# GpSimd's queue in a masked-attention and graph-layer kernel: a block's power goes ahead of the casts that wait for transposes, and the first four casts go out while x is still coming

## The chip, the cores and the metric

The kernel runs on one core of one Trainium2 chip. The metric is the device time of one execution in microseconds (us). Before the change it is 515.58 us, the median of three runs (515.1 to 516.22).

## What is computed

The reference takes x (4096 x 128, float32), a 0/1 matrix adj (4096 x 4096, float32), a scalar beta and a weight (128 x 128):

```python
def L0(x, adj, beta):                     # N = 4096, D = 128
    norm2 = jnp.linalg.norm(x, axis=1, keepdims=True)
    cos = beta[0] * (x @ x.T) / (norm2 @ norm2.T + 1e-07)
    masked = cos + (1.0 - adj) * -1000000000.0
    P = jax.nn.softmax(masked, axis=1)
    return P @ x
def L1(x, edge_index, weight):
    return jnp.matmul(edge_index, jnp.matmul(x, weight))
x = layernorm(x + L0(x, adj, beta))
x = layernorm(x + L1(x, adj, weight))
```

## The kernel before

The 4096 rows are cut into 8 blocks (NB) of 512. For block b the scores against all 4096 columns are made in 16 pairs m = 0 to 15, a pair being two tiles of 128 columns. A pair passes through the engines like this:

- TensorE multiplies the unit rows in three half-precision products for each tile (`scores`, L854 to L856).
- ScalarE takes the exponential (`exp_pair`, L424).
- VectorE masks it with the bytes of adj (`mask_pair`, L639).
- ScalarE writes the upper half-precision part (`split_hi`, L433), and VectorE the rest (`split_lo`, L647).
- TensorE weighs the rows of x with both, three pairs behind the scores (`weigh`, L877 and L881; LAG = 3). A ring of four buffers holds the pairs.

VectorE works in an order written out by hand. In block b it also does the work on the rows of block b-1: it reads the sums at pair 3 (`read_out`, L685), adds the residual rows at pairs 4 and 5 (`residual`, L698, which waits for the transfer of `xres`), takes moments at 6 and 7, makes the variance at pair 8 (`norm_stats`, whose last instruction is L677), and at pair 10 the shift (`row_shift`, L709), which waits for the inverse root of the variance (`rstd_done`).

That inverse root is a `pow` on GpSimd (`power`, L376). GpSimd works in the order of its program as well, and has three kinds of work in it:

- Casts of adj. Each block of adj is four pieces of 512 rows x 1024 columns. `cast(k)` with k = 4b + c issues a DMA from float32 to one byte, DRAM to DRAM (L353). Piece 0 is cut in three (`cast_first(0)` to `cast_first(2)`, L356), which hold the columns of pair 0, pair 1, and pairs 2 and 3. SyncE then issues the DMA that transposes the piece into SBUF (L258 for the first three, L264 for the others). `cast(k)` first waits until the transpose of piece k-2 has landed, so two pieces are under way at a time.
- The powers: four at the start for the norms of x (`inverse_norms(c)`, L360; x comes in four chunks), and one for each block of rows (L376).
- For each block the lower part of the new rows (`x1_split`, L388), after ScalarE's upper part (L469).

At the start VectorE sums the squares of a chunk of x, GpSimd takes the power, VectorE makes the unit rows (`unit_rows`, L530), TensorE turns them, and the pairs of block 0 follow. A mask at the first pair of a piece waits for the piece's transpose. SyncE has its own order: in round b the transposes of block b+1, then the store of the new rows of block b-1 and the load of `xres` for block b (L287), then the store of the parts (L284).

After the last block come the second layer's products (L935, L945), some 125 us, in which no cast is left.

Of the kernel before, what the change touches and what calls it, by code (L numbers as in the profile page):

```python
# [21 lines left out]
def resnorm_graph_kernel(nc, x, adj, beta, weight, x1_dram, x1p_dram, q_dram, adj8_dram, out):  # L22
# [8 lines left out]
    NB = N // BI  # L31
# [9 lines left out]
    NC = 4  # L41
    CT = NT // NC
    MP = 4
# [7 lines left out]
    with ExitStack() as ctx:  # L51
# [3 lines left out]
        def sem(name):  # L55
            return ctx.enter_context(nc.semaphore(name))
# [62 lines left out]
        x_in = [sem(f"x_in{c}") for c in range(NC)]  # L119
# [76 lines left out]
        def piece(v, b, c):  # L196
            return v[b, :, c * PW:(c + 1) * PW]

        def first_piece(v, f):

            c, n = FIRST[f]
            return v[0, :, c * 2 * P:(c + n) * 2 * P]

        def pieces_in(b, c):
            return 16 * (b if c == 0 else b + 1)
# [21 lines left out]
        def chunk(c):  # L227
            return slice(c * CT, (c + 1) * CT)
# [107 lines left out]
        @block.gpsimd  # L336
        def _(pool):
            nc.gpsimd.memset(ident[:, :], 0.0).then_inc(consts, 1)
            nc.gpsimd.memset(xaug[:, :, D:D + 1], 1.0).then_inc(consts, 1)
            nc.gpsimd.memset(half_pow[:, :], -0.5).then_inc(consts, 1)  # L340
            nc.gpsimd.memset(ext[:, :], 0.0).then_inc(consts, 1)
            pool.wait_ge(consts, 4)
            nc.gpsimd.affine_select(out=ident[:, :], in_=ident[:, :], compare_op=ALU.not_equal, fill=1.0,
                                    base=0, pattern=[[-1, P]], channel_multiplier=1).then_inc(consts, 1)

            def cast(k):

                b, c = divmod(k, MP)
                if k < 3:
                    pool.wait_ge(first_in[k], 16)  # L350
                else:
                    pool.wait_ge(piece_in[(k - 2) % MP], pieces_in(*divmod(k - 2, MP)))
                pool.dma_start(piece(adj8_v, b, c), piece(adj_v, b, c)).then_inc(piece_cast[c], 16)  # L353

            def cast_first(f):
                pool.dma_start(first_piece(adj8_v, f), first_piece(adj_v, f)).then_inc(first_cast[f], 16)  # L356

            def inverse_norms(c):
                pool.wait_ge(n2_done, c + 1)
                nc.gpsimd.tensor_tensor(rn[:, chunk(c)], n2[:, chunk(c)], half_pow[:, chunk(c)],  # L360
                                        ALU.pow).then_inc(rn_done, 1)

            inverse_norms(0)

            pool.wait_ge(x_in[NC - 2], 16)
            cast_first(0)
            inverse_norms(1)
            cast_first(1)
            inverse_norms(2)
            cast_first(2)  # L370
            inverse_norms(3)
            for k in range(1, 2 * MP + 2):
                cast(k)
            def power(done, o, n):
                pool.wait_ge(stats_done, done)
                nc.gpsimd.tensor_tensor(rstd[:, o:o + n], rstd[:, o:o + n], half_pow[:, 0:n], ALU.pow).then_inc(rstd_done, 1)  # L376

            for b in range(NB - 1):

                for c in range(2, MP):  # L380
                    if b + 2 < NB:
                        cast((b + 2) * MP + c)
                power(b + 1, 0, IT)
                for c in range(2):
                    if b + 3 < NB:
                        cast((b + 3) * MP + c)
                pool.wait_ge(x1_hi, b + 1)
                nc.gpsimd.tensor_tensor(x1p[:, :, 1, :], x1[:, :, :], x1p[:, :, 0, :],  # L388
                                        ALU.subtract).then_inc(x1_split, 1)
            power(NB, 0, IT)  # L390
            for r in range(NB - 1):
                power(NB + r + 1, IT * (r % 2), IT)
            for half in range(2):
                power(2 * NB + half, IT + half * HT, HT)
# [598 lines left out]
```

## Time and profile before

| | |
|---|---|
| median of the runs | 515.58 us |
| the profiled execution | 515.68 us, its span 513.8 us |
| granted TensorE clock, mean | 0.984 of full speed |
| busy: TensorE, VectorE, ScalarE, GpSimd | 469.7, 380.6, 314.2, 64.8 us |
| chain that ended last | PE 66%, DMA 20%, DVE 4%, issue 4%, ACT 3%, POOL 1% |
| cast transfers | 31 of 512 KB written, median 11.1 us from issue to landing |
| time of the DMA engines | casts 39.5%, SyncE's and the rest of that queue 30.2% of 16 engines' span |

In the profile PE is TensorE, DVE is VectorE, ACT is ScalarE, POOL is GpSimd and SP is SyncE. The span runs from the first to the last instruction. The time of a run is the span and some 2 us around it.

### The profile page before, as it was taken

What the parts mean: (1) busy time and instruction counts of PE and PEld (TensorE: products, weight loads), DVE (VectorE), ACT (ScalarE), POOL (GpSimd) and SP (SyncE); (2) the same over time, 40 slices, a digit from 0 to 9 for tenths busy, and PEclk for the clock granted to TensorE, in tenths of its full rate; (3) what the DMA queues carried; (4) which work ended last, traced back from release to release, by engine and by line L of the source; (5) the groups of instructions that cost most, each with busy time, mean ns of one, the idle gap of its engine ahead of it and who ended that gap; (6) DMA issues with size and microseconds to landing.
All of it is one profiled execution on the core that took longest, in us unless ns stands there. A gap on an engine that the chain in (4) does not pass through costs nothing.

```text
span 513.8 us, 8872 instructions
## 1 busy us (share of the span) xinstructions
PE 469.7 (91%) x3491; PEld 305.1 (59%) x3491; DVE 380.6 (74%) x630; ACT 314.2 (61%) x358; POOL 64.8 (13%) x71
## 2 busy tenths in 40 slices
PE   0866999957999999999999999999999999999995
PEld 0533676635676666766666767666665455544584
DVE  4976989928999999999999999999994022212253
ACT  3665888828879978988988997898891000000000
POOL 3500000010101201201120210110101000000011
PEclk9988999997999999999999999999999999999998
DMA  5899899999999999999989979520024101111111
GB/s 189 62 101 127 86 122 115 137 127 115 172 127 135 131 136 118 131 169 115 112 171 114 105 152 104 93 74 7 1 51 156 63 5 37 41 43 41 42 37 46
DMA packets 101690, 50.20 MB, mean 98 GB/s; under 512 B 69376, under 2 KB 98208, under 8 KB 101664
## 3 DMA queue, kind: packets, MB, share of 16 engines
q0 software_dynamic: 17952, 16.78, 39.5%
q1 hardware_dynamic: 83424, 33.05, 30.2%
q8 instruction: 11, 0.18, 0.1%
q14 instruction: 15, 0.12, 0.1%
q10 hardware_dynamic: 288, 0.07, 0.1%
HBM read 77.40 MB, written 22.82 MB: 195 GB/s over the span
## 4 chain that ended last, share of the span: by engine, by line
PE 66%; DMA 20%; DVE 4%; issue 4%; ACT 3%; POOL 1%; POOLq 0%; ACTq 0%; DVEq 0%
PE psum L935 21%; PE psum L877 16%; DMA adj_bytes<-in_adj 12%; PE psum L881 8%; DMA adjT<-adj_bytes 7%; PE psum L854 7%; PE psum L856 7%; PE psum L855 7%; DVE E L639 2%; ACT E L424 1%; PE psum L945 1%; DMA adjT<-in_x 1%; ACT eh L433 1%; DVE el L647 1%; POOL rn L360 1%
## 5 line engine op out<-in xcount | busy, mean ns | idle before, releaser
L877 PE MATMUL psum<-xaug,eh 128*128 128x257 f16 x1024 | 187.9, 277 | 22.5 <-DVE el L647 15.4
L424 ACT ACTIVATE E<-psum,sc 128x1024 f32<-128x1024 f32 x128 | 154.1, 1204 | 54.8 <-PE psum L856 50.6
L881 PE MATMUL psum<-xaug,el 128*128 128x129 f16 x1024 | 178.7, 223 | 0.0
L639 DVE SCALAR_TENSOR_TENSOR E<-E,adjT 128x1024 f32<-128x1024 f32 x128 | 160.0, 1250 | 21.1 <-ACT E L424 13.0
L647 DVE SCALAR_TENSOR_TENSOR el<-E,eh 128x1024 f16<-128x1024 f32 x128 | 156.5, 1223 | 0.1
L433 ACT ACTIVATE eh<-E 128x1024 f16<-128x1024 f32 x128 | 134.0, 1047 | 3.8 <-DVE E L639 3.8
L877 PEld LDWEIGHTS psum<-xaug,eh 128*128 128x128 f16 x1024 | 100.3, 99 | 52.3 <-DVE el L647 16.9
L935 PE MATMUL psum<-adjT,uT 128*128 128x512 fp8e4 (+1 forms) x576 | 112.1, 355 | 0.0
L881 PEld LDWEIGHTS psum<-xaug,el 128*128 128x128 f16 x1024 | 101.4, 99 | 13.4
L854 PE MATMUL psum<-uT 128*128 (+1 forms) x256 | 98.4, 384 | 0.0
L855 PE MATMUL psum<-uT 128*128 (+1 forms) x256 | 97.8, 382 | 0.0
L856 PE MATMUL psum<-uT 128*128 (+1 forms) x256 | 97.5, 381 | 0.0
L935 PEld LDWEIGHTS psum<-adjT,uT 128*128 128x128 f16 x576 | 56.4, 98 | 53.0
L501 ACT ACTIVATE E<-psum 128x512 f32<-128x512 f32 x7 | 4.2, 597 | 88.0 <-PE psum L935 88.0
L792 DVE TENSOR_TENSOR E<-psum,E 128x512 f32<-128x512 f32 x7 | 4.8, 690 | 68.1 <-PE psum L945 68.1
L376 POOL TENSOR_TENSOR rstd<-rstd,half_pow 128x4 f32<-128x4 f32 (+1 forms) x17 | 22.2, 1304 | 186.1 <-DVE rstd L677 186.1
L353 POOL DMA_DIRECT2D adj_bytes<-in_adj x31 | 19.6, 631 | 192.1 <-DMA adjT<-adj_bytes 192.1
L856 PEld LDWEIGHTS psum<-uT 128*128 128x128 f16 x256 | 25.3, 99 | 31.0 <-issue 1.4
L854 PEld LDWEIGHTS psum<-uT 128*128 128x128 f16 x256 | 25.4, 99 | 17.9 <-issue 0.7
L855 PEld LDWEIGHTS psum<-uT 128*128 128x128 f16 x256 | 25.3, 99 | 16.4 <-issue 0.5
L460 ACT ACTIVATE x<-h,shift,rstd 128x128 f32<-128x128 f32 x32 | 15.2, 482 | 16.6 <-DVE shift L709 16.6
L388 POOL TENSOR_TENSOR x1p<-x,x1p 128x512 f16<-128x512 f32 x7 | 12.4, 1764 | 58.6 <-ACT x1p L469 58.6
(71 smaller groups left out, 159.9 us busy)
## 6 DMA issues: line engine op xcount, KB each, us to landing
adj_bytes<-in_adj POOLq DMA_DIRECT2D x31, 512.0 KB, 11.1
adjT<-in_x SPq DMA_DIRECT2D x4, 512.0 KB, 8.6
xres<-in_x SPq DMA_DIRECT2D x8, 256.0 KB, 5.3
q_row<-norms SPq DMA_DIRECT2D x8, 256.0 KB, 4.9
x_rows<-x SPq DMA_DIRECT2D x8, 256.0 KB, 3.6
E<-x_rows SPq DMA_DIRECT2D x8, 256.0 KB, 3.0
out<-E SPq DMA_DIRECT2D x16, 128.0 KB, 2.2
x_parts<-x1p SPq DMA_DIRECT2D x7, 256.0 KB, 5.5
```

What stands on the lines that cost most here:

```text
L353: pool.dma_start(piece(adj8_v, b, c), piece(adj_v, b, c)).then_inc(piece_cast[c], 16)
L376: nc.gpsimd.tensor_tensor(rstd[:, o:o + n], rstd[:, o:o + n], half_pow[:, 0:n], ALU.pow).then_inc(rstd_done, 1)
L424: nc.scalar.activation(E[:, m % RING, :, :], S[m % 2], ACT.Exp, bias=col(C_BB), scale=col(C_BS)).then_inc(e_done, 1)
L433: nc.scalar.activation(eh[:, m % RING, :, :], E[:, m % RING, :, :], ACT.Copy, scale=ECAST).then_inc(hi_done, 1)
L639: nc.vector.scalar_tensor_tensor(out=e, in0=e, scalar=EPRE, in1=mask_bytes(b, m), op0=ALU.mult, op1=ALU.min).then_inc(masked, 1)
L647: nc.vector.scalar_tensor_tensor(out=el[:, s, :, :], in0=E[:, s, :, :], scalar=ECAST, in1=eh[:, s, :, :], op0=ALU.mult, op1=ALU.subtract). ...
L854: nc.tensor.matmul(o, hj, hi, start=True, stop=False)
L855: nc.tensor.matmul(o, hj, li, start=False, stop=False)
L856: last = nc.tensor.matmul(o, lj, hi, start=False, stop=True)
L877: return nc.tensor.matmul(O[t][:, 0:XC], eh[:, s, a, cols], xaug[:, j, :], start=start, stop=stop)
L881: return nc.tensor.matmul(O[t][:, 0:D + 1], el[:, s, a, cols], xaug[:, j, 0:D + 1], start=False, stop=False)
L935: last = nc.tensor.matmul(out, x1p_all[:, j, part * D:(part + 1) * D], adj_cols(r, j, cols), start=j == 0 and part == 0, stop=j == NT - 1 ...
```

## The change

Two places of GpSimd's program change, and nothing else.

At the start GpSimd waits for the second chunk of x where it had waited for the third, and this wait and two of the first casts now stand ahead of the first power. The third of the first casts and `cast(1)` follow that power; `cast(1)` no longer waits for the transpose of the pair-1 columns.

In the loop over the blocks the power of block b stands ahead of `cast` for pieces 2 and 3 of block b+2, where it had stood behind them. The casts themselves, their order and their waits stay.

```diff
             def cast(k):
                 b, c = divmod(k, MP)
-                if k < 3:
+                if k == 2:
                     pool.wait_ge(first_in[k], 16)
-                else:
+                elif k > 2:
                     pool.wait_ge(piece_in[(k - 2) % MP], pieces_in(*divmod(k - 2, MP)))
                 pool.dma_start(piece(adj8_v, b, c), piece(adj_v, b, c)).then_inc(piece_cast[c], 16)
...
+            pool.wait_ge(x_in[1], 16)
+            cast_first(0)
+            cast_first(1)
             inverse_norms(0)
-
-            pool.wait_ge(x_in[NC - 2], 16)
-            cast_first(0)
+            cast_first(2)
+            cast(1)
             inverse_norms(1)
-            cast_first(1)
             inverse_norms(2)
-            cast_first(2)
             inverse_norms(3)
-            for k in range(1, 2 * MP + 2):
+            for k in range(2, 2 * MP + 2):
                 cast(k)
...
             for b in range(NB - 1):
-                for c in range(2, MP):
-                    if b + 2 < NB:
-                        cast((b + 2) * MP + c)
+
                 power(b + 1, 0, IT)
-                for c in range(2):
-                    if b + 3 < NB:
-                        cast((b + 3) * MP + c)
+                for k in range((b + 2) * MP + 2, (b + 3) * MP + 2):
+                    if k < NB * MP:
+                        cast(k)
                 pool.wait_ge(x1_hi, b + 1)
                 nc.gpsimd.tensor_tensor(x1p[:, :, 1, :], x1[:, :, :], x1p[:, :, 0, :],
                                         ALU.subtract).then_inc(x1_split, 1)
```

## Rows read from the trace of the kernel before

**Rows 1.** The waits of the whole span: engine, line, releaser, total us, times, longest.

```profile
DVE shift L709 <- POOL rstd L376: 11.4, 2, 10.3
DVE E L639 <- DMA adjT<-adj_bytes: 7.7, 1, 7.7
```

**Rows 2.** VectorE's timeline, 64 to 145 us: start, length, what, idle before.

```profile
83.87 0.75 DVE L685 TENSOR_TENSOR h<-psum,o_lo 128x256 f32<-128x256 f32 x2
...
100.98 0.16 DVE L677 TENSOR_TENSOR rstd<-tmp 128x4 f32<-128x4 f32 x1
...
115.95 0.16 DVE L709 SCALAR_TENSOR_TENSOR shift<-mean,rstd 128x4 f32<-128x4 f32 x1 [10.27 <-POOL rstd L376]
...
137.66 0.74 DVE L685 TENSOR_TENSOR h<-psum,o_lo 128x256 f32<-128x256 f32 x2
...
143.06 0.60 DVE L698 SCALAR_TENSOR_TENSOR h<-h,rden,xres 128x128 f32<-128x128 f32 x2
```

**Rows 3.** VectorE's timeline, 175 to 186 us.

```profile
180.22 0.75 DVE L685 TENSOR_TENSOR h<-psum,o_lo 128x256 f32<-128x256 f32 x2
```

**Rows 4.** GpSimd's timeline, 0 to 70 us.

```profile
9.75 1.66 POOL L360 TENSOR_TENSOR rn<-n,half_pow 128x8 f32<-128x8 f32 x1 [8.04 <-DVE n L526]
11.35 0.81 POOL L356 DMA_DIRECT2D adj_bytes<-in_adj  x1
12.19 2.32 POOL L360 TENSOR_TENSOR rn<-n,half_pow 128x8 f32<-128x8 f32 x1
...
43.50 0.62 POOL L353 DMA_DIRECT2D adj_bytes<-in_adj  x1 [15.07 <-DMA adjT<-adj_bytes]
```

**Rows 5.** The chain of work that ended last, in order of time: start, length, what.

```profile
14.48 3.90 DMA adj_bytes<-in_adj
...
24.98 10.62 DMA adj_bytes<-in_adj
35.62 7.60 DMA adjT<-adj_bytes
```

**Rows 6.** VectorE's timeline, 0 to 64 us.

```profile
14.54 1.23 DVE L530 SCALAR_TENSOR_TENSOR adjT<-adjT,rn 128x1024 f32<-128x1024 f32 x1
...
43.31 1.23 DVE L639 SCALAR_TENSOR_TENSOR E<-E,adjT 128x1024 f32<-128x1024 f32 x1 [7.67 <-DMA adjT<-adj_bytes]
```

**Rows 7.** ScalarE's timeline, 0 to 64 us.

```profile
36.97 1.20 ACT L424 ACTIVATE E<-psum,sc 128x1024 f32<-128x1024 f32 x1 [3.99 <-PE psum L856]
```

**Rows 8.** TensorE's timelines, 9 to 60 us and 100 to 125 us.

```profile
46.92 0.39 PE L877 MATMUL psum<-xaug,eh 128*128 128x257 f16 x1 [4.86 <-DVE el L647]
...
118.44 0.40 PE L877 MATMUL psum<-xaug,eh 128*128 128x257 f16 x1 [8.86 <-DVE el L647]
```

**Rows 9.** Windows: stretch, its us, busy us of each engine, granted clock, DMA share, GB/s.

```profile
10.00:28.00 18.00, 12.34 (x59) 7.70 (x59) 17.15 (x54) 13.07 (x33) 10.44 (x9) 1.00 0.78 74
28.00:60.00 32.00, 22.82 (x167) 15.33 (x168) 23.78 (x22) 20.70 (x21) 1.66 (x3) 0.89 1.07 114
47.00:50.00 3.00, 3.00 (x18) 2.21 (x19) 3.00 (x3) 1.82 (x2) 0.00 (x0) 0.50 1.09 100
```

**Rows 10.** GpSimd's timeline, 60 to 520 us.

```profile
75.74 0.61 POOL L353 DMA_DIRECT2D adj_bytes<-in_adj  x1 [12.53 <-DMA adjT<-adj_bytes]
...
95.19 0.61 POOL L353 DMA_DIRECT2D adj_bytes<-in_adj  x1 [1.16 <-DMA adjT<-adj_bytes]
...
114.87 1.04 POOL L376 TENSOR_TENSOR rstd<-rstd,half_pow 128x4 f32<-128x4 f32 x1
...
155.01 1.95 POOL L376 TENSOR_TENSOR rstd<-rstd,half_pow 128x4 f32<-128x4 f32 x1 [3.31 <-DVE rstd L677]
...
226.49 0.64 POOL L353 DMA_DIRECT2D adj_bytes<-in_adj  x1 [10.50 <-DMA adjT<-adj_bytes]
...
240.15 1.95 POOL L376 TENSOR_TENSOR rstd<-rstd,half_pow 128x4 f32<-128x4 f32 x1 [10.34 <-DVE rstd L677]
```

**Rows 11.** SyncE's timeline, 64 to 145 us.

```profile
129.49 0.43 SPq L287 DMA_DIRECT2D xres<-in_x  x1
```

**Rows 12.** The page's DMA issues: count, KB each, median us to landing.

```profile
xres<-in_x SPq DMA_DIRECT2D x8, 256.0 KB, 5.3
```

## The prediction, made before the changed kernel ran

> **What bounds the kernel now.** I read the page's chain first (TensorE 66%, DMA 20%), then the waits, then the timelines of the engines around each long one. In steady state TensorE sets the pace: the read-out of a block's sums comes at 137.66 and the next at 180.22 [rows 2, 3], so a block takes 42.56 us, 2.66 a pair. The DMA share of the chain lies all before 115 us, and two waits of VectorE stand there [rows 1]:
>
> - Stall A, in block 0: the mask of pair 4 waits 7.67 us, until 43.31, for the transpose of piece 1 [rows 6]. Its cast was issued at 24.98, took 10.62, and the transpose 7.60 [rows 5].
> - Stall B, in block 1: the shift of pair 10 waits 10.27 us, until 115.95, for the power [rows 2]. Its input had been made at 100.98. GpSimd came to it only at 114.87 [rows 10], because two casts stood ahead of it that waited for transposes. Nothing else was missing.
>
> Later blocks have neither: there GpSimd reaches the power before VectorE has the variance, and idles for it (3.31 and 10.34 us [rows 10]).
>
> **Stall B: the power first.** The price of stall B is read from the blocks, not from the wait. Between the read-outs of blocks 0 and 1 lie 137.66 - 83.87 = 53.79 us [rows 2] against 42.56 without a stall: 11.2 us. That is 8.9 us in which TensorE stood [rows 8], and a rest for the half clock behind it and a slow mask. All of it goes if the power comes in time. After the change GpSimd's casts 2 to 9 still precede this power; the last of them went out at 95.19, done by 95.8 [rows 10], and not later with a stream that starts sooner. With stall A's gain below (4.1) the variance is made at 96.9, the power is done 1.95 us later [rows 10] at 98.9, and VectorE asks for it at 105.68 - 4.1 = 101.6. Cover: 2.7 us. Gain 11.2; bounds 10.3 (the wait alone) and 11.8.
>
> The row of the power itself says something too: 1.04 us while VectorE stood waiting, 1.95 while it worked [rows 10]; I charge the longer one. The Trainium skill ("SBUF — State Buffer", section "Who interferes with whom") says that a GpSimd instruction that reads SBUF and a VectorE one with two SBUF inputs shut each other out. By it the power may wait out one mask; the cover still holds, and the sum is the same. The same page's warning, that casts issued by GpSimd can starve for descriptors while VectorE holds the pair, speaks against the first four casts; it is priced as a rival.
>
> **What the moved casts lose.** The casts now stand behind the power, so behind its wait for the variance; behind them wait the transposes and the lower part of the new rows. In blocks 1 and 2 the variance comes 15 us sooner (155.01 gives 139.7), before the next cast is free to go, so nothing is held. From block 3 it holds: cast 22 went out at 226.49, and its power runs at 240.15 - 15.3 = 224.9, done at 226.8 [rows 10]. With the stream 5 us sooner the cast could go at 221.5, so it loses some 5 us. The piece is then ready at 226.8 + 18.2 (10.62 + 7.60 [rows 5]) = 245.0. Its mask is pair 8 of block 5, two blocks and five pairs after 180.22, less 15.3: 263.3. Cost 0. If that cover were gone it would cost 5 us.
>
> **Stall A: the start.** Three terms.
>
> 1. The powers for the norms come later. The second chunk of x is there at about 9.4 (an estimate: VectorE's and ScalarE's work on it begins between 9.4 and 9.6; the first power's 9.75 bounds it from above). Then two issues of 0.81 and 0.61 to 0.7 [rows 4, 10], the first power of 1.66 [rows 4], two more issues, and the second power of 2.32 [rows 4]: 9.4 + 1.5 + 1.7 + 1.4 + 2.3 = 16.3. The second unit rows began at 14.54 [rows 6], right when that power ended. VectorE has no gap worth the name from there to pair 4, so all of block 0 starts 1.8 us later. Bounds 1.0 and 2.6 (all powers at their short, or long, length).
> 2. Piece 1 comes sooner. Its cast goes out at 13.9 instead of 24.98. The DMA engines were at share 0.78 from 10 to 28 us and at 1.07 when full [rows 9], so the idle time that can be filled is 18 x 0.29 / 1.07 = 4.9 us, and I take the whole stream 5 us sooner: piece 1 at 43.2 - 5 = 38.2. It can be more (7), since piece 1 no longer shares with piece 2 from its start. From below, 2 us, the lead of the first cast (11.35 [rows 4] to 9.4).
> 3. What is late next is not the mask's place in VectorE's order but the exponential of pair 4. It ran from 36.97 to 38.17 [rows 7], because TensorE had just come out of a wait. Shifted by 1.8 it ends at 40.0, later than piece 1. So the mask gains 43.31 - 40.0 = 3.3 and not 7.7. For TensorE: the weighing that restarted at 46.92 [rows 8] waits for three VectorE instructions of 1.2 to 1.3 us from the mask on, so without the DMA it was free at 38.2 + 3.8 = 42.0, 4.9 sooner; the 3 us at half clock (1.2 GHz) behind that pause [rows 9] cost 1.5 more; some 0.5 is given back, as VectorE, with two extra instructions for x in these pairs, is just slower than TensorE there. 4.9 + 1.5 - 0.5 - 1.8 = 4.1.
>
> Are the next pieces there? Piece 4 (block 1, pair 0) let cast 6 go at 75.74 [rows 10], so was ready at 75.45. Its mask is three pairs before 83.87, at 75.9; it had 0.4 us to spare. After: needed at 71.8, ready at 70.4. Piece 8 (block 2) was cast before 95.19, so ready by 113.4, less 5; needed at 137.66 - 15.3 - 8.0 = 114.4. From there on 42.6 us a block leave the stream ahead.
>
> `xres` of block 1's rows is the other close one. SyncE issues it behind four transposes, at 129.49 [rows 11]; after, 124.5. With the median of 5.3 [rows 12] it lands at 129.8, and the residual wants it at 143.06 - 15.3 = 127.8 [rows 2]. That is 2 us late, of which TensorE feels what exceeds the 1.4 us between VectorE's wait in stall B and its own (10.27 against 8.86 [rows 2, 8]): 0.6, and nothing if the stream gains 7. I put 0.
>
> **Sum.** 4.1 + 11.2 = 15.3 us. The profiled execution took 515.68, so 500.4; the median of the runs is 0.1 lower, which I ignore: 500.4.
>
> **Rivals.**
>
> - The stream is late again (or `xres` is). If it comes only 2 us sooner, piece 1 is ready at 41.2 (1.2 late) and piece 4 at 73.4 against 71.8; `xres` at 132.8 against 127.8, 5 late, 3.6 of them felt. Together up to 5: 501.5 to 505. For it: piece 4 had 0.4 to spare, and the three wants lie within 2 us of supply. Against: the idle DMA time at the start is there to be filled.
> - The start gains more: shift 1.0, B at its upper bound: 498.3 to 499.3. For it: pieces early; against: VectorE is full there.
> - Only one stall goes, because a new wait fills the other: gain 4.1 to 10.5, 505 to 511.5. For it only the closeness above.
> - Nothing moves: the power still stands behind something. Then 515.6. The order of the program speaks against it.
> - Slower: the fourth cast in a row doesn't leave GpSimd until room is made, the other powers stand behind it, and the start slides. Casts ahead of it were never more than two under way, so no row shows four. Held for h us, the time is 500.4 + h. It decides from h = 15.3, about when piece 1's own cast would land (13.9 + 10.62, and up to 5 for the two ahead): then 516 to 518. Against it: each issue of the trace took 0.6 to 0.8.
>
> **How the numbers follow.** Forecast with its own range 499.3 to 501.5: 0.60. Stream or `xres` late: 0.22. More at the start: 0.07. One stall only: 0.06. Nothing: 0.02. Slower: 0.03. Faster by over 0.2% (1 us, about what a measurement of this kernel can tell) 0.95, within it 0.02, slower 0.03. The range 498.3 to 505 leaves out the last three and little else.
>
> **What would show it.** Right: VectorE's wait for the power in block 1 is gone; 42.6 between all read-outs; read-out of block 0 at 79.8, of block 1 at 122.4; the second unit rows near 16.3; the mask of pair 4 waits for ScalarE and not for a DMA; the first four issues within 5 us. Wrong: a wait of a mask for a transpose at pairs 4, 12 or the first of block 1, a wait of the residual for `xres`, an issue on GpSimd over 1 us, or a power before 17 us that is longer than 2.4.

## The result, and the profile after

The changed kernel takes 507.2 us (median of 4 runs, 505.87 to 509.05) against 515.34 for the kernel before: ratio 0.9848, interval 0.9801 to 0.9894. It is faster, but by half of what was forecast (500.4), and outside the range. Run again later (experiment 8) the same program took 503.82 (502.4 to 505.02), ratio 0.9792 (0.976 to 0.9824). In both together its runs spread from 502.4 to 509.05. Two slow executions among the experiments, one of 1007.18 us in the second and one of 508.53 in the fifth, are left out of the medians and ratios given there.

The profiled execution took 508.47 us, its span was 506.7. First the waits of the whole span: engine, line, releaser, total us, times, longest. VectorE's lines after the change stand one lower than before; the power of GpSimd, L376 before, is L377.

```profile
DVE h L697 <- DMA xres<-in_x: 3.4, 1, 3.4
DVE E L638 <- DMA adjT<-adj_bytes: 2.2, 1, 2.2
```

VectorE's wait for the power in block 1 is gone [rows 1]; so is pair 4's for piece 1. Two others are new. VectorE's timeline shows where (start, length, what, idle before):

```profile
14.42 1.23 DVE L529 SCALAR_TENSOR_TENSOR adjT<-adjT,rn 128x1024 f32<-128x1024 f32 x1 [0.25 <-POOL rn L360]
...
24.98 1.23 DVE L638 SCALAR_TENSOR_TENSOR E<-E,adjT 128x1024 f32<-128x1024 f32 x1 [2.25 <-DMA adjT<-adj_bytes]
...
41.11 1.22 DVE L638 SCALAR_TENSOR_TENSOR E<-E,adjT 128x1024 f32<-128x1024 f32 x1 [3.27 <-ACT E L423]
...
80.68 0.75 DVE L684 TENSOR_TENSOR h<-psum,o_lo 128x256 f32<-128x256 f32 x2
...
123.25 0.75 DVE L684 TENSOR_TENSOR h<-psum,o_lo 128x256 f32<-128x256 f32 x2
...
133.11 0.61 DVE L697 SCALAR_TENSOR_TENSOR h<-h,rden,xres 128x128 f32<-128x128 f32 x2 [3.41 <-DMA xres<-in_x]
...
167.24 2.17 DVE L638 SCALAR_TENSOR_TENSOR E<-E,adjT 128x1024 f32<-128x1024 f32 x1 [0.27 <-ACT E L423]
...
170.47 0.74 DVE L684 TENSOR_TENSOR h<-psum,o_lo 128x256 f32<-128x256 f32 x2
...
252.43 2.65 DVE L646 SCALAR_TENSOR_TENSOR el<-E,eh 128x1024 f16<-128x1024 f32 x1
```

The read-outs of the eight blocks, before and after, are the account of the whole change:

| interval between read-outs | before | after | after, again |
|---|---|---|---|
| (read-out of block 0) | 83.87 | 80.68 | 79.55 |
| 0 to 1 | 53.79 | 42.57 | 42.57 |
| 1 to 2 | 42.56 | 47.22 | 43.17 |
| 2 to 3 | 42.57 | 43.17 | 43.33 |
| 3 to 4 | 42.57 | 43.64 | 43.17 |
| 4 to 5 | 42.57 | 43.40 | 43.58 |
| 5 to 6 | 42.57 | 42.56 | 42.57 |
| 6 to 7 | 40.49 | 40.64 | 40.45 |

Stall B gives 11.2 us, as forecast. The read-out of block 0 comes 3.2 sooner (how much of that is the start's doing, experiment 1 shows). Then 4.65 us are lost in one interval and 0.6, 1.1 and 0.8 in the next three: 7.2 us lost, against 14.4 won.

GpSimd's timeline and a line of SyncE's show what lies at these places:

```profile
98.04 1.94 POOL L377 TENSOR_TENSOR rstd<-rstd,half_pow 128x4 f32<-128x4 f32 x1 [8.97 <-DVE rstd L676]
...
144.95 1.95 POOL L377 TENSOR_TENSOR rstd<-rstd,half_pow 128x4 f32<-128x4 f32 x1 [18.74 <-DVE rstd L676]
146.88 1.31 POOL L353 DMA_DIRECT2D adj_bytes<-in_adj  x2
164.50 0.61 POOL L353 DMA_DIRECT2D adj_bytes<-in_adj  x1 [16.30 <-DMA adjT<-adj_bytes]
166.52 0.62 POOL L353 DMA_DIRECT2D adj_bytes<-in_adj  x1 [1.41 <-DMA adjT<-adj_bytes]
167.16 1.17 POOL L387 TENSOR_TENSOR x1p<-x,x1p 128x512 f16<-128x512 f32 x1
```

```profile
122.57 0.43 SPq L287 DMA_DIRECT2D xres<-in_x  x1
```

Casts 14 and 15 go out back to back at 146.88, right behind the power: neither waited for its transpose any more, they had been held. Casts 16 and 17 wait for their transposes, and the subtraction for the lower part of the new rows (L387), last in the queue, starts at 167.16. ScalarE had made the upper part, all that it needs, at 160.8. The subtraction starts 0.08 us ahead of a mask, and that mask takes 2.17 us instead of 1.22. The read-out follows at 170.47, one `split_lo` later.

In the kernel before, ScalarE itself released the subtraction in these blocks. There, too, it made a mask longer, but that mask stood 7.5 us ahead of the read-out at 180.22, and the interval was 42.57 all the same. VectorE's timeline of the kernel before:

```profile
172.68 1.83 DVE L639 SCALAR_TENSOR_TENSOR E<-E,adjT 128x1024 f32<-128x1024 f32 x1 [0.27 <-ACT E L424]
```

In the changed kernel the instructions beside the subtraction in the next three intervals took 1.82, 2.65 and 2.06 us, 0.6, 1.4 and 0.8 over the usual 1.22, and the intervals are 0.6, 1.1 and 0.8 too long.

### The profile page after: what moved, and what is told of

It is laid out like the page before. It is cut to its first block, busy times and chain, and to the rows that moved or that the text cites. A ratio compares the mean times of both kernels' runs of the same rounds, so it can differ in the third digit from the quotient of the medians.

```text
span 506.7 us, 8872 instructions
## 1 busy us (share of the span) xinstructions
PE 467.8 (92%) x3491; PEld 303.3 (60%) x3491; DVE 382.3 (75%) x630; ACT 315.2 (62%) x358; POOL 62.2 (12%) x71
## 4 chain that ended last, share of the span: by engine, by line
PE 60%; DMA 24%; DVE 7%; issue 3%; ACT 3%; SPq 1%; POOL 1%; POOLq 0%; ACTq 0%; DVEq 0%
PE psum L934 21%; DMA adj_bytes<-in_adj 15%; PE psum L876 13%; PE psum L880 7%; DMA adjT<-adj_bytes 6%; PE psum L855 6%; PE psum L854 6%; PE psum L853 6%; DVE el L646 3%; DVE E L638 2%; DMA xres<-in_x 2%; PE psum L944 1%; DMA adjT<-in_x 1%; ACT E L423 1%; ACT eh L432 1%
## 5 line engine op out<-in xcount | busy, mean ns | idle before, releaser
L880 PE MATMUL psum<-xaug,el 128*128 128x129 f16 x1024 | 176.9, 222 | 0.0
L646 DVE SCALAR_TENSOR_TENSOR el<-E,eh 128x1024 f16<-128x1024 f32 x128 | 159.1, 1243 | 0.0
L377 POOL TENSOR_TENSOR rstd<-rstd,half_pow 128x4 f32<-128x4 f32 (+1 forms) x17 | 23.1, 1359 | 246.1 <-DVE rstd L676 246.1
L831 PE MATMUL psum<-ident,adjT 128*128 128x128 f32 x32 | 6.2, 351 | 13.6 <-DVE adjT L529 13.6
```

Of the source, the lines that this page charges most:

```text
L646: nc.vector.scalar_tensor_tensor(out=el[:, s, :, :], in0=E[:, s, :, :], scalar=ECAST, in1=eh[:, s, :, :], op0=ALU.mult, op1=ALU.subtract). ...
L880: return nc.tensor.matmul(O[t][:, 0:D + 1], el[:, s, a, cols], xaug[:, j, 0:D + 1], start=False, stop=False)
```

## The experiments

All ratios are to the kernel before, run beside it on the same chip. Experiments 1, 2, 3 and 5 were run together, then 4, 6, 7 and 8, then 9 to 12. The expectations of experiments 1 and 2 speak of GpSimd's "multiply" for the lower part; it is the subtraction. The intervals given are those up to the read-out of block 6; the last one is 40.4 to 40.8 us in every trace.

**1. The loop alone.** The start is put back word for word:

```diff
-            pool.wait_ge(x_in[1], 16)
-            cast_first(0)
-            cast_first(1)
             inverse_norms(0)
-            cast_first(2)
-            cast(1)
+            pool.wait_ge(x_in[NC - 2], 16)
+            cast_first(0)
             inverse_norms(1)
...
```

> The start is that of the kernel before; only the loop over the blocks has the power ahead of four casts. Theory (the gain of stall B is given back by the residual rows' transfer and by GpSimd's multiply for the lower part falling on a full stretch of VectorE): the wait for the power in block 1 is gone, the wait of pair 4 in block 0 for its piece stays at 7.7 us, read-out of block 0 at 83.9; the residual of block 1's rows waits 2 to 6 us for its transfer (issued near 129.5, wanted near 131.9); the read-outs of blocks 3 to 5 follow each other at 43.0 to 43.7 us instead of 42.6. Time 505 to 509 us, a gain of 7 to 10. Rival (nothing is given back, the loss of the changed kernel is all in the start): no wait for the transfer, all read-outs at 42.6, time 504.2, a gain of 11.2.

506.99 us, ratio 0.9848 (0.9823 to 0.9873). Intervals 42.57, 44.05, 44.4, 43.5, 42.57, 43.57: all that stall B cost is won, and much is given back. The residual waited in three blocks, 2.16, 1.00 and 1.35 us; the load of the first was issued at 126.87, behind a stream that was late as before. The read-out of block 0 came at 80.35, not 83.9: x arrived 1.6 us sooner than in the profile of before, and pair 4 waited 5.86 us. So when x comes in scatters by 1.6 us (the first clamp of the norms ran at 9.50 before, at 7.9 in the traces of the changed kernel and of this one), and with x equally soon the old start has its read-out at 80.35, no later than the changed kernel's 80.68. None of the 3.2 us is shown to be the start's.

**2. The start alone.**

```diff
             for b in range(NB - 1):
-                power(b + 1, 0, IT)
-                for k in range((b + 2) * MP + 2, (b + 3) * MP + 2):
+                for c in range(2, MP):
+                    if b + 2 < NB:
+                        cast((b + 2) * MP + c)
+                power(b + 1, 0, IT)
+                for c in range(2):
...
```

> The start is the changed one; the loop is that of the kernel before, with two casts ahead of each power. Theory: the first mask waits some 2 us for the transpose of the first columns, read-out of block 0 comes 2 to 3 us sooner than before; casts 10 and 11 go out at 104 to 106, so the power is done near 108 and VectorE waits some 5 us for it instead of 10.3; from block 2 on all read-outs at 42.6, since GpSimd's multiply comes where it came before; time 506 to 509.5. Rival (the start gives back what it brings, and the gain of the changed kernel is the loop's alone): within 2 us of before, 513 to 515.5.

503.99 us (501.89 to 505.02), ratio 0.9802 (0.977 to 0.9833): the start alone gains about what both parts gained together (0.9848 and 0.9792). Its waits, 20 to 200 us, and GpSimd's timeline, 95 to 105 us:

```profile
DVE shift L710 <- POOL rstd L377: 2.2, 1, 2.2
DVE E L640 <- DMA adjT<-adj_bytes: 1.2, 1, 1.2
```

```profile
98.14 0.62 POOL L353 DMA_DIRECT2D adj_bytes<-in_adj  x1 [14.71 <-DMA adjT<-adj_bytes]
102.01 0.62 POOL L353 DMA_DIRECT2D adj_bytes<-in_adj  x1 [3.25 <-DMA adjT<-adj_bytes]
102.64 1.05 POOL L377 TENSOR_TENSOR rstd<-rstd,half_pow 128x4 f32<-128x4 f32 x1
```

The casts that stood ahead of the power (111.59 and 114.24 in the kernel before) go out 12 to 13 us sooner (1.6 of it is x's earlier arrival), and of stall B's 10.3 us only 2.2 are left, with the power still in its old place. The intervals are 44.3 and then 42.56 to 42.58. My expectation had 5 us left. The two parts of the change heal the same stall, and only the loop's part lengthens the blocks behind it.

**3. The residual rows' load ahead of the last transpose of a round.**

```diff
                 for c in range(MP):
...
+                    if c == MP - 1 and ahead_of_last is not None:
+                        store_x1(ahead_of_last - 1)
+                        load_xres(ahead_of_last)
                     sp.wait_ge(piece_cast[c], pieces_in(b, c))
...
```

> The changed kernel, with SyncE issuing the store of the new rows and the load of the residual rows ahead of the last of the four transposes of a round, not behind it. Theory (the residual's wait of 3.4 us and most of the 4.7 us that block 2 is too long are this transfer): no wait of the residual, read-outs of blocks 1 and 2 at 42.6 to 43.6 instead of 47.2, a gain of 3 to 4.5 us on the changed kernel, 503 to 504.5. Rival (with the wait gone the ring's slack or a late piece takes its place, or the transfer lands as late because the engines are full): a gain under 1 us, and either a wait of the residual that stays, or a mask that waits for a transpose in block 2.

502.08 us, ratio 0.9759 (0.9735 to 0.9784). No wait of the residual; the second interval is 42.7. The later ones stay long (43.28, 42.88, 43.32): the second loss is another.

**4. The subtraction ahead of the last two casts.**

```diff
                 power(b + 1, 0, IT)
-                for k in range((b + 2) * MP + 2, (b + 3) * MP + 2):
+                for k in range((b + 2) * MP + 2, (b + 3) * MP):
                     if k < NB * MP:
                         cast(k)
                 pool.wait_ge(x1_hi, b + 1)
                 nc.gpsimd.tensor_tensor(x1p[:, :, 1, :], ...)
+                for k in range((b + 3) * MP, (b + 3) * MP + 2):
+                    if k < NB * MP:
+                        cast(k)
```

> The changed kernel, with GpSimd's multiply-free subtraction for the lower part of the new rows (L387) moved ahead of the last two of the four casts of a block; the power stays ahead of all four. Theory (blocks 3 to 5 are 0.6 to 1.1 us too long because this subtraction, queued behind four held casts, starts within 4 us of the read-out and stops VectorE where it has no slack): it starts right behind ScalarE's upper part, some 13 us ahead of the read-out, and the read-outs from block 3 on follow each other at 42.6; 2 to 3 us less than the changed kernel in the same call, the residual's wait of block 2 unchanged. Rival (the held casts themselves disturb the blocks, by bunching the transfers): the read-outs stay at 43.2 to 43.7 although the subtraction has moved, and the time stays.

500.59 us, ratio 0.9722 (0.9694 to 0.9751), 3.2 us under the changed kernel run beside it. GpSimd's timeline, then VectorE's:

```profile
155.58 1.87 POOL L387 TENSOR_TENSOR x1p<-x,x1p 128x512 f16<-128x512 f32 x1 [12.72 <-ACT x1p L471]
...
183.53 1.30 POOL L353 DMA_DIRECT2D adj_bytes<-in_adj  x2
```

```profile
121.68 0.74 DVE L687 TENSOR_TENSOR h<-psum,o_lo 128x256 f32<-128x256 f32 x2
...
155.21 1.22 DVE L649 SCALAR_TENSOR_TENSOR el<-E,eh 128x1024 f16<-128x1024 f32 x1
156.70 1.83 DVE L641 SCALAR_TENSOR_TENSOR E<-E,adjT 128x1024 f32<-128x1024 f32 x1 [0.27 <-ACT E L426]
...
164.25 0.75 DVE L687 TENSOR_TENSOR h<-psum,o_lo 128x256 f32<-128x256 f32 x2
...
206.82 0.75 DVE L687 TENSOR_TENSOR h<-psum,o_lo 128x256 f32<-128x256 f32 x2
```

The casts are held as before (two in a row at 183.53), yet the intervals are 42.57 but for one of 43.14. The subtraction now waits for ScalarE and takes 1.87 us instead of 1.17. The `split_lo` that was running keeps its 1.22; the mask behind it takes 1.83. So VectorE gives up 0.6 us here too, but as in the kernel before, 8.7 us from the subtraction's start to the read-out, and the interval doesn't show it. The residual waited 0.63 us in one block and 1.11 in another; the second is in the interval of 43.14.

**5. cast(1) behind all four powers for the norms.** The edit moves `cast(1)` but does not give it back its old wait, as the expectation has it: `cast` is the changed kernel's, and this one went out at 18.84, right behind the last power.

> The changed kernel, with cast(1) behind the four powers for the norms and with its old wait for the pair-1 columns' transpose; the first three casts stay early. Theory (the first mask waits 2.25 us because the transposes of the first columns share the DMA engines with cast(1), which is queued before them): the transpose of the first columns lands within 4 to 6 us of its issue instead of 11.4, no wait of the first mask, pair 4's mask still not held by its piece, and a gain of 1.5 to 2.5 us on the changed kernel, 504.7 to 505.7. Rival (the third cast or x itself fills the engines): the first mask waits as long, and the time is that of the changed kernel or, with piece 1 late, 1 to 4 us more.

505.03 us (500.3 to 505.07), ratio 0.9766 (0.9705 to 0.9827), too wide to tell from the changed kernel. The mechanism shows in VectorE's timeline:

```profile
41.33 1.23 DVE L637 SCALAR_TENSOR_TENSOR E<-E,adjT 128x1024 f32<-128x1024 f32 x1 [3.63 <-DMA adjT<-adj_bytes]
```

The transpose of the first columns landed 6.0 us after its issue, the first mask waited for no transpose, but pair 4 waited 3.6 us for piece 1. Half of the theory and half of the rival held: cast(1) does crowd out the first transposes, and this place is too late for it. x came late in this trace, as in that of the kernel before.

**6. The power first in the first block only.**

```diff
+                if b == 0:
+                    power(b + 1, 0, IT)
                 for k in range((b + 2) * MP + 2, (b + 3) * MP):
                     if k < NB * MP:
                         cast(k)
+                if b > 0:
+                    power(b + 1, 0, IT)
+                for k in range((b + 3) * MP, (b + 3) * MP + 2):
...
```

> The changed kernel, but only the first block's power goes ahead of the casts; from the second on two casts stand ahead of it as in the kernel before. Theory (the power's wait holds the stream by 7 us from block 2 on, and with it all that is queued behind): casts 14 and 15 go out at 138 to 141 and not at 147, the subtraction follows ScalarE from block 3 on, read-outs at 42.6 from there; 2 to 3 us less than the changed kernel in the same call. The wait for the residual rows in block 2 stays, as it lies ahead of this difference. Rival (the powers come late again without their place): a wait of VectorE for the power in block 2 or 3, and the time of the changed kernel or more.

501.87 us, ratio 0.9759 (0.9733 to 0.9785), 2.0 under the changed kernel run beside it. Casts 14 and 15 went out at 136.0 and 138.5, the subtraction came at 156.9, and the intervals are 43.18, where the subtraction still stands right behind casts, and then 42.56 to 42.57. No power came late in these blocks, and the wait for the residual rows that the expectation had kept didn't come.

**7. Experiments 3 and 6 together.**

> The power ahead of the casts in the first block only, and the residual rows' load ahead of the last transpose of a round. Theory (the two losses are separate, 4 to 5 us for the transfer and 2 to 3 for the held casts): all read-outs at 42.6 to 42.9, 499.5 to 501 us, less than the kernel with the load moved alone (502.1). Rival (they overlap, or one shifts into the other): 502 or more.

503.96 us, ratio 0.9795 (0.9771 to 0.9819): a miss, and the rival held. In SyncE's order the last transpose of a round now stands behind the store, which waits for the finished rows. GpSimd's timeline:

```profile
164.60 0.62 POOL L357 DMA_DIRECT2D adj_bytes<-in_adj  x1 [7.32 <-DMA adjT<-adj_bytes]
165.24 1.46 POOL L397 TENSOR_TENSOR x1p<-x,x1p 128x512 f16<-128x512 f32 x1
```

The held transpose holds cast 17, and the subtraction falls at 165.24, against a read-out at 165.60. Intervals from the second on: 43.19, 42.57, 42.7, 43.3, 44.12. In the last of these VectorE also waited 1.49 us for a power.

**8. The changed kernel again.**

> The changed kernel once more, word for word, as the measure for the others of this call. Theory (its loss is the residual's wait plus the subtraction's place): 505.9 to 509; in this trace again a wait for the residual rows of 1 to 4 us in block 2 and read-outs of 43.1 to 43.7 us in blocks 3 to 5. Rival (the first trace was a chance one): no such wait, and a time within 1 us of 502.

503.82 us. Its trace has the second loss (43.17 to 43.58 in four intervals, 3.0 us in all) and not the first: the load was issued at 119.4, landed 8.4 later, and nobody waited. Neither the theory's wait nor the rival's 502 came; the wait for the residual comes and goes.

**9. The subtraction cut to one element a partition.** The lower parts of seven blocks' rows are left out but for one column of one tile, and are zero.

```diff
+            nc.gpsimd.memset(x1p[:, :, :, :], 0.0).then_inc(consts, 1)
+            pool.wait_ge(consts, 6)
...
-                nc.gpsimd.tensor_tensor(x1p[:, :, 1, :], x1[:, :, :], x1p[:, :, 0, :],
+                nc.gpsimd.tensor_tensor(x1p[:, 0, 1, 0:1], x1[:, 0, 0:1], x1p[:, 0, 0, 0:1],
                                         ALU.subtract).then_inc(x1_split, 1)
```

> The changed kernel with GpSimd's subtraction for the lower part of the new rows cut to one element a partition (so the lower parts of the first seven blocks' rows are left out, all but one column of one tile, and are zero), in the same place, with the same waits, behind the same held casts. Theory (blocks 2 to 5 are too long because the full subtraction stops VectorE just ahead of the read-out): the held casts stay, but the read-outs of blocks 3 to 5 follow each other at 42.6, and no VectorE instruction near a read-out takes 2 us; 499.5 to 502. Rival (the held and bunched transfers do it): read-outs stay at 43.2 to 43.6, 502.5 to 505.

502.27 us (500.51 to 505.28), ratio 0.979 (0.9738 to 0.9841). The times scatter too much to say, the trace says it:

```profile
183.54 1.32 POOL L353 DMA_DIRECT2D adj_bytes<-in_adj  x2
...
203.28 0.62 POOL L353 DMA_DIRECT2D adj_bytes<-in_adj  x1 [2.06 <-DMA adjT<-adj_bytes]
203.91 0.42 POOL L389 TENSOR_TENSOR x1p<-x,x1p 128x1 f16<-128x1 f32 x1
```

```profile
164.26 0.75 DVE L686 TENSOR_TENSOR h<-psum,o_lo 128x256 f32<-128x256 f32 x2
...
206.84 0.75 DVE L686 TENSOR_TENSOR h<-psum,o_lo 128x256 f32<-128x256 f32 x2
```

Held casts, bunched transfers, the same place 3 us ahead of the read-out, and all intervals at 42.57 or 42.58, in the one traced execution (500.51). So it is the subtraction's length there, and not the held casts, that lengthens the blocks.

**10. The subtraction as in 4, and the load in the middle of a round.**

```diff
+                    if c == 2 and ahead_of_third is not None:
+                        sp.wait_ge(stats_done, ahead_of_third)
+                        load_xres(ahead_of_third)
                     sp.wait_ge(piece_cast[c], pieces_in(b, c))
...
-                load_xres(b)
+                if b + 1 == NB:
+                    load_xres(b)
...
```

> The subtraction ahead of the last two casts (as in the fourth experiment) and the residual rows' load issued between the second and third transpose of a round, as soon as the block's variance is made, so no transpose is held for it. Theory (the two losses are separate and both go): every read-out from block 0 on at 42.6, no wait of the residual, 498.5 to 500 us. Rival (the load in the middle of the round delays a transpose, as the load moved ahead of the last one did): some read-outs at 43 or more, 500.6 or above.

500.33 us (499.25 to 500.96), ratio 0.9736 (0.97 to 0.9773). All intervals from block 0 on 42.56 to 42.58, no wait of the residual. Both losses are gone; the median is a little above the 500 expected, and not clearly below experiment 4 (0.9722), which left the load where it was.

**11. As 10, with cast(1) behind the third of the norms' powers.**

```diff
             cast_first(2)
-            cast(1)
             inverse_norms(1)
             inverse_norms(2)
+            cast(1)
             inverse_norms(3)
```

> As the tenth, and cast(1) behind the third of the norms' powers instead of ahead of the second, some 4 us later. Theory (the first mask waits 1.2 to 2.3 us, since the first columns' transposes share the engines with cast(1)): that wait falls under 0.5 us, pair 4's mask waits at most 1 us for piece 1, and the time is 1 us under the tenth's. Rival (piece 1 is then late by what the first mask gains, as when cast(1) stood behind all four): pair 4's mask waits 1 to 3.6 us for a transpose, and the time is the tenth's or more.

498.41 us (498.16 to 498.96), ratio 0.9693 (0.9658 to 0.9729): the fastest version here, and the one with the least scatter. Its median is 1.9 us under the tenth's, but of that the two traces show 0.4, at the read-out of block 0 (78.39 against 78.77). VectorE's timeline:

```profile
22.39 1.20 DVE L645 SCALAR_TENSOR_TENSOR E<-E,adjT 128x1024 f32<-128x1024 f32 x1
...
38.82 1.22 DVE L645 SCALAR_TENSOR_TENSOR E<-E,adjT 128x1024 f32<-128x1024 f32 x1 [3.42 <-ACT E L430]
```

The first mask waits for nothing, and pair 4's for the exponential, not for a transpose.

**12. The changed kernel with only the load moved, as in 10.**

> The changed kernel with only the residual rows' load moved, as in the tenth; the subtraction stays behind four casts. Theory (the residual's wait comes and goes from run to run of the changed kernel and costs up to 4 us when it is there; the subtraction's place costs 2.5 to 3 always): no wait of the residual, read-outs of blocks 3 to 5 at 43.1 to 43.6 as before, 501.5 to 503, with less scatter between runs than the 505.9 to 509 and 502.4 to 505 of the changed kernel. Rival (the scatter has another source): the same scatter, 3 us or more from lowest to highest.

503.41 us (502.78 to 504.9), ratio 0.9795 (0.9754 to 0.9836). No wait of the residual; intervals 44.17, 43.17, 43.16, 43.17, then 42.56. With the subtraction behind four casts 3.4 us stay lost, and the median lies just above the range expected. The scatter is 2.1 us, between the two expectations.

## Why the prediction was wrong

The mechanism that was to gain did gain; what it gives back was put at nothing in two places, and the two gains were taken for independent.

- **Stall B, 11.2 us: right.** The interval fell from 53.79 to 42.57, and the power was done at 99.98, close to the forecast 98.9, ahead of VectorE.
- **"What the moved casts lose", put at 0: wrong; this step failed in every trace of the changed kernel.** It asked only whether the held piece is ready for its mask, which it is, by far. It named the lower part of the new rows as queued behind and did not ask when it would run. In the first trace it starts 2 to 4 us sooner than before (167.16 against 171.56, 297.36 against 299.27), while the read-outs come 7 to 10 us sooner: so it falls 3.3 to 4.5 us ahead of the read-outs of blocks 2 to 5 instead of 8.7, and what it takes from VectorE isn't made up by the read-out. Price: 2.5 us in three intervals of the first trace and a part of the 4.65 in the interval ahead of them, 3.0 in the second trace, 0 where it was moved (experiment 4) or cut short (9). The step was wrong, too, in saying that nothing is held in blocks 1 and 2: casts 14 and 15 were free at about 139 and 141 (casts 12 and 13 at 121.68 and 124.29, and some 17 us) and went at 146.88.
- **The residual rows, put at 0: mis-sized, and named as a rival.** The text had the load late by 2 us, took off 1.4 for what TensorE doesn't feel, and let the rest vanish in the hope of an earlier stream. Measured in the first trace: the load was issued at 122.57, sooner than the forecast 124.5; mis-sized was its way to landing, 10.4 us where the median of 5.3 had been taken (8.4 in the second trace). The wait was 3.41, and with two VectorE instructions that the subtraction stretched to 2.19 and 2.17 us the interval came out 4.65 too long. Experiment 3 took it away and gained 5.1 us on the changed kernel's first median, 1.7 on its second. In six other traces with the load unmoved and the start changed (2, 4, 5, 6, 8, 9) the waits in all were 0, 1.7, 1.9, 0, 0 and 0.6. It is a race that the changed kernel sometimes loses; why the transfer took 10.4 us once is not shown. Nor is it shown that this alone makes its runs scatter (502.4 to 509.05): experiment 12 has no such wait and still 2.1 us of scatter.
- **Stall A and the start, 4.1: too much.** At the early arrival of x there are ten traces with the changed start, whose read-out of block 0 comes at 78.77 to 80.68, and one with the old start, 80.35 (experiment 1): from 0.3 us later to 1.6 sooner. At the late arrival there are only the kernel before, 83.87, and experiment 5, whose `cast(1)` stands later, 80.90; so what the start is worth in block 0 isn't settled. The first term held: the second unit rows began at 14.42 against 12.95 in experiment 1, 1.5 us later where 1.8 was forecast. The exponential did take the place of the DMA, as forecast (41.11, wait on ScalarE). Missed was the first mask: its transpose, issued at 13.53, landed 11.4 us later, because the casts issued behind its own filled the engines (with `cast(1)` later it landed after 6.0 and 6.7, experiments 5 and 11), and the mask waited 2.25. The text filled the idle DMA time without asking whom that slows. The stream's lead itself was if anything larger than the 5 us that I took: with x equally soon, cast 3 went out at 32.99 and 31.47 in the two traces of the changed kernel against 40.97 in experiment 1, and cast 12 at 121.68 and 119.07 against 126.98.
- **The sum.** 4.1 + 11.2 adds two parts that overlap. Experiment 2, by the start alone, takes 8.1 of stall B's 10.3 us; it gains 10.2 us (ratio 0.9802), experiment 1 gains 7.8, and both together 7.8 to 10.7. The start's worth shows in block 1, not in block 0, where I had booked it.

The mechanism of the rival "stream or `xres` late" held for the first trace, with 3.4 of wait where it had up to 5; its time, 501.5 to 505, fits the second. The rival on the slower side, a GpSimd that can't issue a fourth cast, is refuted: the first four issues took 0.61 to 0.72 us each. "Only one stall goes" gave the right time, 505 to 511.5, and half of the reason: block 0 gained little, and a new wait stood there, but most of the rest was lost in the blocks behind.

## What to carry to other kernels

When an instruction is moved ahead in an in-order queue, follow everything behind it to its new place on the clock of the other engines, not only the pieces with a deadline: work that nobody waits for can still hurt by when it runs. Before adding two gains, ask whether one of them already shortens the wait that the other removes; running each half alone costs two runs and showed it here at once. And where idle transfer time is filled early, look at the short transfers that were landing in it.

## What the runs showed of the hardware

GpSimd's subtraction with its inputs in SBUF and a VectorE instruction with two SBUF inputs don't work side by side: where they meet, one of them or both take longer. Issued right behind a cast, the subtraction took 1.17 to 1.69 us over all traces (experiment 9's small one apart), and where it took 1.17 or 1.18 in the first trace the VectorE instruction beside it took 2.17, 2.65 and 2.06. Released by ScalarE, it took 1.86 or 1.87 in every one of them.

In experiment 4 the `split_lo` that was running when ScalarE released it kept its 1.22 and the mask behind it took 1.83. The starts alone don't tell which of the two is stopped: the `split_lo` of 252.43 began 0.38 us ahead of a subtraction and took 2.65, the one of experiment 4 began 0.37 ahead and kept its 1.22. Why is open. That the two exclude each other is the rule of the Trainium skill ("SBUF — State Buffer", section "Who interferes with whom") which the prediction had applied to the power and not to the subtraction in the same queue; the trace agrees.

The transpose of the first 128 KB landed 3.6 us after its issue in the kernel before, 11.4 and 11.5 in the two traces of the changed one with four casts issued ahead of it, 6.7 us with cast(1) some 4 us later (experiment 11), and 6.0 with cast(1) last (5).
